# The second mixture of a four-layer kernel: two sends signalled apart, fill products ahead of and during the first fetch, first rows rounded in halves, and the dense expert by 512 columns

## The reference, cut to what matters

```
logits = xf @ w_g
topv, topi = top_k(logits, 2)
full = full_like(logits, -1e9).at[arange(N)[:, None], topi].set(topv)
probs = softmax(full)
capacity = 640                       # int(2 * 1.25 * 2048 / 8)
rank = cumsum(one_hot(topi)) - 1     # first choices of all tokens, then second ones
mask = mask * (rank < capacity)
exp_batches = einsum('nec,nd->ecd', sec_mask, xf)
h = gelu(einsum('ecd,edh->ech', exp_batches, c_fc))    # 128 -> 512
exp_out = einsum('ech,ehd->ecd', h, c_proj)            # 512 -> 128
out = einsum('nec,ecd->nd', cb, exp_out)
```

## Time and profile before

| | before |
|---|---|
| median of 3 runs | 578.73 us (578.64 to 579.26) |
| the profiled execution | 577.52 us |
| its span, first to last instruction | 575.7 us |
| PE busy | 492.8 us (86%) |
| DVE busy | 323.8 us (56%) |
| POOL busy | 242.2 us (42%) |
| ACT busy | 241.1 us (42%) |

### The profile page before, as it was taken

How to read it: one execution, slowest core, us unless ns; L and a number is a source line. 1 busy time by engine, 2 the same in 40 slices (tenths; PEclk the granted TensorE clock), 3 DMA queues, 4 the chain that set the end, 5 groups by cost and what they waited for, 6 DMA issues and landing times.

```text
span 575.7 us, 9196 instructions
## 1 busy us (share of the span) xinstructions
PE 492.8 (86%) x3294; PEld 396.8 (69%) x3294; DVE 323.8 (56%) x1125; ACT 241.1 (42%) x477; POOL 242.2 (42%) x354
## 2 busy tenths in 40 slices
PE   2799893779779977987995499999899899999997
PEld 2558483769456726684884299998653778799997
DVE  4866427845896733688741146642775944433334
ACT  2653744324245541345560054421545295344440
POOL 5771866455335012366777515663760340000000
PEclk9799897559758997995598699999999999999999
DMA  9999710311850066700011212113500000000002
GB/s 279 336 201 206 249 58 12 99 38 32 291 172 1 0 172 166 213 1 0 29 52 49 83 54 81 40 37 126 179 2 0 2 1 2 0 1 1 1 2 73
DMA packets 56861, 48.04 MB, mean 83 GB/s; under 512 B 6082, under 2 KB 47240, under 8 KB 56688
## 3 DMA queue, kind: packets, MB, share of 16 engines
q1 hardware_dynamic: 53728, 42.06, 26.2%
q0 software_dynamic: 2656, 4.88, 2.7%
q10 hardware_dynamic: 432, 0.52, 0.3%
HBM read 35.21 MB, written 12.82 MB: 83 GB/s over the span
## 4 chain that ended last, share of the span: by engine, by line
PE 60%; DVE 24%; POOL 6%; issue 5%; DMA 3%; ACT 2%; ACTq 0%; POOLq 0%; DVEq 0%; SPq 0%
PE ps L1248 10%; PE ps L1186 6%; DVE st L1628 5%; PE ps L1069 4%; PE ps L1071 4%; PE ps L1070 4%; POOL tok L2309 3%; PE ps L822 3%; PE ps L709 3%; PE ps L752 3%; PE ps L762 2%; DVE mv L1631 2%; PE ps L845 2%; PE ps L825 2%; DVE mx L1666 2%
## 5 line engine op out<-in xcount | busy, mean ns | idle before, releaser
L2058 DVE SCALAR_TENSOR_TENSOR x<-ps,gate,x 128x128 f32<-128x128 f32 x128 | 36.0, 344 | 54.8 <-PE ps L1248 54.8
L1248 PEld LDWEIGHTS ps<-moe_w,big 128*128 128x128 f32 x512 | 61.1, 192 | 3.9 <-issue 1.7
L1515 ACT ACTIVATE big<-ps,col 128x512 f32<-128x512 f32 x64 | 42.2, 689 | 48.2 <-PE ps L1071 48.1
L1248 PE MATMUL ps<-moe_w,big 128*128 128x128 f32 x512 | 61.4, 275 | 0.9 <-DVE x L2047 0.9
L2400 POOL DMA_INDIRECT res<-qT,dest x43 | 42.2, 981 | 41.2 <-DVE qT L2033 26.7
L709 PE MATMUL ps<-con,xn 128*128 128x128 f32 x148 | 29.3, 332 | 28.1 <-ACT xn L1451 15.3
L1507 ACT ACTIVATE big<-ps 128x320 f32<-128x320 f32 x56 | 24.3, 439 | 59.2 <-PE ps L1071 59.0
L709 PEld LDWEIGHTS ps<-con,xn 128*128 128x128 f32 x148 | 20.5, 171 | 38.8 <-DVE xn L1646 34.8
L2199 POOL TENSOR_SCALAR rstd<-mv 128x4 f32<-128x4 f32 x36 | 9.2, 256 | 80.5 <-DVE mv L1631 79.5
L1363 ACT ACTIVATE xT<-ps 128x512 f32<-128x512 f32 x41 | 24.1, 590 | 45.2 <-PE ps L709 45.2
L1186 PE MATMUL ps<-moe_w,big 128*128 128x128 f32 x344 | 41.3, 275 | 0.6 <-ACT big L1507 0.6
(11 more groups left out here) (345 smaller groups left out, 1197.7 us busy)
## 6 DMA issues: line engine op xcount, KB each, us to landing
ring<-in_ew SPq DMA_DIRECT2D x20, 256.0 KB, 4.7
moe_w<-in_m0w SPq DMA_DIRECT2D x16, 256.0 KB, 6.2
moe_w<-in_m2w SPq DMA_DIRECT2D x16, 256.0 KB, 5.8
tok<-zero SPq DMA_DIRECT2D x1, 2580.0 KB, 27.7
big<-tok SPq DMA_DIRECT2D x7, 322.5 KB, 2.8
res<-zero SPq DMA_DIRECT2D x1, 2048.0 KB, 28.6
moe_w<-in_ew SPq DMA_DIRECT2D x8, 256.0 KB, 5.7
big<-res SPq DMA_DIRECT2D x4, 512.0 KB, 5.7
```

What stands on the lines that cost most here:

```text
L1248: last = mm(ps[7 - i % 2 if i >= B else 6 + i % 2][:, cols(c)], big[:, FC * (e % 2) + f, i % B, cols(c)], w[:, e, F + P * f:F + P * f + P] ...
L1515: A(big[:, 2 * (e % 2) + f, t, :], bank[:, :], ACT.Gelu, bias=V("m3b1", 2 * e + f)).then_inc(h_act, 1)
L2058: last = v.scalar_tensor_tensor(out=x[:, C * t + c, :], in0=bank[:, cols(c)], scalar=gate[:, C * t + c, e:e + 1], in1=x[:, C * t + c, :], ...
```

## The change

- **Sends.** The last two of the 32 sends count on a semaphore of their own (`sent_last`, which is `r_ld[1]`). SP and POOL wait for both, as before for the one. PE waits for the first 30 sends, issues 9 constant products, waits for the last two, issues 10 more, and 4 more after the first transposes.
- **First rows.** The first expert's five transposes go two to `ps0` and three to `ps1`. DVE rounds and subtracts the first 256 columns, ACT rounds the other 384, DVE subtracts them. Each half has its own signal, and the first expert's products and gelus are of 256 and 384 columns instead of 320 and 320. The transposes of the second group no longer wait for the whole of DVE's first group, only for both halves.
- **Dense expert.** The first layer is one fp32 product of 512 columns per unit instead of three fp32r passes. The second layer of tiles 0 to 2 is 4 products of 512 columns instead of 16 of 128, which leaves it by dimension. Hence 12 transposes (`whole_turned`) bring it back, and DVE adds it to `x` straight from PSUM (`whole_add`), all of it ahead of the first fetch. Tile 3 keeps the old second layer. ACT's four roundings of `x`, DVE's four remainders and POOL's split of expert 0's weights are gone.
- **Count.** DVE sums the 16 first-choice matrices (`oh_sum`), and PE multiplies the sum once instead of 16 products.
- Two small ones: `minus_half` is merged into `zeroed`, and four diagonals move from `xT` to `kr_w`.

```diff
+LAST = 2
+SENT = 16 * (2 * B * C - LAST + 2)
+SENT_LAST = 16 * (LAST + 2)
...
             def count_second():
-                for c in range(nb):
-                    mm(ps[1][:, 0:(nb + 1) * E], ones[:, :], bc(oh[:, c, :], [P, nb + 1, E], [1]), start=c == 0, stop=False)
                 pe.wait_ge(oh_ready, 2 * B + 1)
+                mm(ps[1][:, 0:(nb + 1) * E], ones[:, :], bc(oh_sum[:, :], [P, nb + 1, E], [1]), start=True, stop=False)
...
                 def hidden(t):
-                    pe.wait_ge(low_ready, t + 1)
+                    if not late:
+                        pe.wait_ge(xT_ready, turns(rows, t))
                     for f in range(4):
                         if t >= 1:
                             pe.wait_ge(h_act, n["h"] - 3)
-                        product(ps[2 + f][:, :], w1_high["m2"][:, 0, cols(f)], w1_low["m2"][:, 0, cols(f)],
-                                qTR[:, t, :], whole_low[:, t % 2, :])
+                        elif f % 2:
+                            pe.wait_ge(xT_ready, turns(rows, (f + 1) // 2))
+                        mm(ps[2 + f][:, :], moe_w[:, 0, cols(f)], xT[:, t, :], start=True, stop=True).then_inc(h_mm, 1)
...
+                def results_by_dim(t, units):
+                    for f in range(4):
+                        last = mm(ps[6 + t % 2][:, :], moe_w[:, 0, 512 + P * f:512 + P * f + P], hid[:, t % 2, f, 0:S],
+                                  start=f == 0, stop=f == 3)
...
+            def whole_turned():
+                for t in range(B - 1):
+                    pe.wait_ge(gy_sb, done0["whole"] + min(t + 2, B - 1))
+                    if t >= 2:
+                        pe.wait_ge(whole_added, t - 1)
+                    for c in range(C):
+                        last = nc.tensor.transpose(ps[7 - t % 2][:, cols(c)], whole_y[:, C * t + c, :], ident)
+                    last.then_inc(whole_tok, 1)
...
                 if name == "m2":
+                    whole_turned()
                     pe.wait_ge(sent, SENT)
-                    keep_busy(ps[7], BUSY // 2 + 2)
+                    keep_busy(ps[2], BUSY // 2 + 2)
+                    pe.wait_ge(sent_last, SENT_LAST)
+                    keep_busy(ps[2], BUSY // 2 + 3)
...
                 turn_group(0)
+                if name == "m2":
+                    keep_busy(ps[2], 4)
                 units = hidden(0)
...
+            def whole_add(t):
+                dve.wait_ge(whole_tok, t + 1)
+                for c in range(C * t, C * t + C):
+                    i = v.scalar_tensor_tensor(out=x[:, c, :], in0=ps[7 - t % 2][:, cols(c - C * t)], scalar=have[:, c:c + 1], in1=x[:, c, :],
+                                               op0=ALU.mult, op1=ALU.add)
+                i.then_inc(whole_added, 1)
...
+                    if name == "m2" and g == 0:
+                        link(v.tensor_copy(xg_high[:, 0, 0:FIRST], ps[0][:, 0:FIRST]))
+                        v.tensor_tensor(xg_low[:, 0, 0:FIRST], ps[0][:, 0:FIRST], xg_high[:, 0, 0:FIRST].bitcast(F32), ALU.subtract).then_inc(gT_s, 1)
+                        dve.wait_ge(first_high, 1)
+                        v.tensor_tensor(xg_low[:, 0, FIRST:], ps[1][:, 0:a["cap"] - FIRST], xg_high[:, 0, FIRST:].bitcast(F32), ALU.subtract).then_inc(gT_s, 1)
...
                 if name == "m2":
+                    act.wait_ge(gT_m, PLACED["m0"]["groups"] + 1)
+                    A(xg_high[:, 0, FIRST:], ps[1][:, 0:a["cap"] - FIRST], ACT.Identity).then_inc(first_high, 1)
...
-                                      oob_is_err=False).then_inc(sent, 16)
+                                      oob_is_err=False).then_inc(sent if j < 2 * B * C - LAST else sent_last, 16)
```

More of the change, by code:

```diff
@@ L369, in build @@
         oh = sb("oh", [P, 2 * B * C, E], BF16)
+        oh_sum = sb("oh_sum", [P, E], BF16)
         tri = sb("tri", [P, P], BF16)
@@ L544, in build @@
             a["N"] = a["cap"] // a["pieces"]
+        FIRST, HALVES = 2 * P, 2
+        piece = lambda name, i, j: slice((0, FIRST)[j], (FIRST, PLACED[name]["cap"])[j]) if name == "m2" and i == 0 else slice(j * PLACED[name]["N"], (j + 1) * PLACED[name]["N"])
         done0["last"] = done0["m2"] + PLACED["m2"]["n"] * PLACED["m2"]["nb"]
@@ L1075, in whole_expert @@
                 pe.wait_ge(loaded, 32 * E)
-                pe.wait_ge(split, 8)
-                pe.wait_ge(x_high, B)
+                rows = n["turn"] - 1
                 def hidden(t):
-                    pe.wait_ge(low_ready, t + 1)
+                    if not late:
+                        pe.wait_ge(xT_ready, turns(rows, t))
                     for f in range(4):
@@ L1101, in whole_expert @@
                 if late:
-                    results(B - 1, hidden(B - 1))
+                    results_by_token(B - 1, hidden(B - 1))
                     return
@@ L1161, in hidden @@
                                 pe.wait_ge(h_act, n["h"] - 3)
-                            tokens = slice(at + j * N, at + (j + 1) * N)
+                            tokens = slice(at + piece(name, i, j).start, at + piece(name, i, j).stop)
+                            N = tokens.stop - tokens.start
                             if name == "m2":
+                                if i == 0 and f == 0:
+                                    pe.wait_ge(gT_s, g0 - HALVES + j + 1)
                                 high, low = w1_high[name][:, e, cols(f)], w1_low[name][:, e, cols(f)]
@@ L1183, in results @@
                             pe.wait_ge(gy_sb, done0[name] + q - 1)
+                        if q < 2 and name == "m2":
+                            pe.wait_ge(whole_added, B - 1)
                         o = ps[6 + q % 2][:, cols(0)]
@@ L1218, in stage @@
                     if t == 0:
-                        pe.wait_ge(split, 16)
+                        pe.wait_ge(split, PLACED["m2"]["n"] + E)
                     for f in range(2):
@@ L1360, in stage @@
                         A(xT[:, t, :], ps[2 * t + 1][:, :], ACT.Identity).then_inc(xT_ready, 1)
-                        A(qTR[:, t, :], ps[2 * t + 1][:, :], ACT.Identity).then_inc(x_high, 1)
                     else:
@@ L1987, in group @@
                         dve.wait_ge(h_mm, units0[name] + 4 * a["pieces"] * eg * (g - 1))
-                    for j in range(0, gb_, 4):
+                    if name == "m2" and g == 0:
[3 more added lines that the diff above has]
+                        v.tensor_tensor(xg_low[:, 0, FIRST:], ps[1][:, 0:a["cap"] - FIRST], xg_high[:, 0, FIRST:].bitcast(F32), ALU.subtract).then_inc(gT_s, 1)
+                    for j in range(gb_ if name == "m2" and g == 0 else 0, gb_, 4):
                         m = min(4, gb_ - j)
@@ L2105, in _ @@
             second_largest(False)
+            with_sum = oh[:, 0:nb, :].rearrange("p c e -> p e c")
+            with nc.allow_low_precision(reason="whole numbers up to 16"):
+                v.tensor_reduce(oh_sum[:, :], with_sum, AX.X, ALU.add)
             first_largest(lg2[:, :, :], oh[:, nb:2 * nb, :], slice(0, nb))
@@ L2127, in _ @@
             link(v.tensor_tensor(have[:, 0:nb], gb[:, 0:nb, 0], gb[:, nb:2 * nb, 0], ALU.add))
-            whole_low_of(2)
-            whole_out(0)
-            whole_low_of(3)
-            for t in range(1, B - 1):
+            for t in range(B - 1):
                 whole_out(t)
             prepared("L3")
+            for t in range(B - 1):
+                whole_add(t)
+            dve.wait_ge(whole_added, B - 1)
             evacuate("m2", 1)
@@ L2259, in stage @@
                         for e in (2 * t, 2 * t + 1):
-                            split_expert(mix, w, width, e)
+                            if name == "L3" or e >= PLACED["m2"]["whole"]:
+                                split_expert(mix, w, width, e)
                 return stage
@@ L2406, in _ @@
             g_.memset(attT[:, :], 0.0).then_inc(zeroed, 1)
-            g_.memset(half[:, :], -0.5).then_inc(minus_half, 1)
-            pool.wait_ge(minus_half, 1)
+            g_.memset(half[:, :], -0.5).then_inc(zeroed, 1)
+            pool.wait_ge(zeroed, 3)
             pool.wait_ge(ld_c, 32)
```

61 lines of the change are left out of this document (30 added, 31 removed).

## The result

The changed kernel took 575.66 us, median of 5 runs (574.72 to 577.50), the kernel before 578.64 us (5 runs, 578.30 to 579.26). The ratio is 0.9948, with a 95% interval of 0.9925 to 0.9972: 3.0 us faster. The forecast was 576.1 us, 575.0 to 578.1.

A forecast was written before the change was run, and what follows sets the result against it. POOL's sends bound the kernel up to 321.8 us, then PE. A 3.3 us earlier second group less 0.6 for tile 3 gave 2.7 us: 578.73 - 2.7 = 576.03, forecast 576.1 us, range 575.0 to 578.1.

The forecast's parts named there:

- Sends and transposes: Second mixture's start: fill begins after the 30th send, clock rises 4.0 us later, transposes start at 325.4 against 325.67.
- the lower bound: Transposes behind the last send: no earlier than 325.0, because of the fetch; the second group then gains 3.7 us.
- The late rise: Rival at the fill: clock rises 2 to 3 us later, net gain 1.2 to 1.7 us, 577.2; chance 0.17.
- the bound 326.9: Transposes' start if the rise comes 3 us later: 16.4 products are slow, the second group gains 1.8 us.
- First rows: First expert's halves: first product at about 327.1 against 328.89, second group 3.3 us earlier.
- Dense expert: Tiles 0 to 2: 24 products take 20.6 us against 19.2, PE free before 319.3; effect taken as zero.
- the rival: Whole dense stage at 1.2 GHz: free until PE comes after 321.3; all 24 products slow, near 587; chance 0.05.
- Tile 3: Dense expert's last tile: four fp32 products take 3.44 us against 2.86, so 0.6 us is taken off the gain.
- The rest at zero: Roundings, remainders, split and 15 counting products lie beside POOL's chain of sends: zero gain.
- Sum: Whole kernel: 3.3 - 0.6 = 2.7 us gained.
- What would have shown it wrong: Signs include transposes later than 4.5 us behind the landing, or first sum less than 2 us earlier.
- listed for right: Signs include fill 2.5 us before the landing, first product about 5.4 behind it, first sum released by constant products.

The follow-up runs named there:

- clock-kept kernels: Changed kernel with 8 more constant products ahead of the wait for the 30th send: 575.17 us, ratio 0.9929; three variants of this: 0.9944, 0.9929, 0.9925.
- the second profile of the changed kernel: Changed kernel run again with no edit, against the kernel before: 576.64 us, ratio 0.9942.
- dense edit alone: Changed kernel with the second mixture's start as before, also called dense edit only: 579.73 us, ratio 1.0019 to the kernel before.
- Count only: Kernel before with one summed one-hot in place of the sixteen counting products: 580.94 us (1 run).
- dense edit only, again: Second timing of the changed kernel with the second mixture's start as before: 579.28 us, ratio 0.9997 to the kernel before.
- one signal: Changed kernel with 9 constant products behind the signal of all 32 sends, instead of 9 and 10 behind two signals: 577.54 us, ratio 0.9971 to before.
- rows whole: Changed kernel with the first group of rows rounded whole and products of 320 columns: 576.86 us, ratio 0.9967 to the kernel before.

## Why the prediction was right, step by step

**Sends and transposes: right, at the lower bound.** The rise came 3.2 us after the start of the fill where I took 4.0, and the transposes stood 3.08 us behind the landing where I took 3.6 (325.4 against 321.82). The clock-kept kernels show that the bound of the fetch, 325.0 or 3.2 us, was well read: 2.97 to 3.05. What the step did not weigh enough is that the fill is a bet: started slow, nineteen products ended 3.08, 3.34, 4.48 or 5.17 us behind the landing in four profiles.

**The late rise: a rival that happened, in single executions.** I gave it 0.17 and the bound 326.9, which is 5.1 behind the landing; the second profile of the changed kernel has 5.17. It costs 2.1 us in the sum. How many of the timed runs had it is not known, since only a profiled one shows the moment. The spread of the runs is not explained by it: the first profile, with the early rise, is of the slowest of its five runs. The Trainium skill, TensorE: Matmul & The Clock Gate, Part 1, gives half a microsecond either way for the moment; the runs here spread from 2.7 to 5.8 us behind the start of the constant products, so the measurement decides against that figure for this place.

**First rows: right.** The halves take 1.75 us from transposes to first product (I had 1.7, before 3.22). Idle time ahead of the first product is 0.18 us (0.2 to 0.3). The products of the first expert run at 0.12 to 0.18 us. The second group is 3.68 us earlier where the sum had 3.3: the term was 0.4 too small, and that is the half microsecond of the transposes.

**Dense expert: mechanism right.** Windows of the changed kernel's first profile, where it starts at 292.64:

```profile
293.00:294.00 1.00, 1.00 (x2) 0.46 (x2) 0.93 (x5) 0.28 (x1) 0.97 (x1) 0.50 0.20 66
294.00:295.00 1.00, 1.00 (x2) 0.32 (x1) 0.90 (x5) 0.27 (x1) 0.70 (x1) 0.62 0.20 66
```

The clock was low for its first 2.1 us, as feared in the rival, and it took 21.7 us to the key products (23.2 in the first profile of the dense edit alone) against 20.6 at full clock. PE was still through at 319.0, 3.2 us before it was wanted. Tile 3 costs 0.58 us more, as predicted 0.6. The estimate from the Trainium skill's four passes (FP8 and Floating Point Precision, TensorE Precision Notes) was 0.95, and the trace does not bear it out. Of these 0.58 only 0.33 came off the gain: tile 3 starts 3.83 us earlier and the first sum 3.50. Before, the fetch set the first sum, and PE had the rest to spare. The term was 0.3 too large.

**The rest at zero: wrong by 0.3 us,** the step "lie beside POOL's chain of sends: zero". One send of 1.35 us becomes 0.97. Count only shows that the summed count alone does it, by moving DVE against POOL; in the changed kernel DVE's subtractions, beside which the send was long, are gone as well, so there either edit could be the cause.

**Sum.** 3.5 us behind the landing and 0.3 ahead of it, in place of 2.7. The medians say 3.0 [0.28% to 0.75%, 1.6 to 4.3 us]. The rest, 0.8 us, is less than executions differ by elsewhere. That the median fell within 0.4 us of the forecast is in part luck: at the loop, at tile 3 and at the sends the working left out 0.3 to 0.4 us of gain each, all to the same side, and the two profiles of the changed kernel gained 3.5 and 1.4 us behind the landing.

**One price was added up wrongly,** that of the rival in which the whole dense stage is slow. If 9.5 us of lateness eat the whole gain, 20.6 us leave 11.1 on top of 578.7, near 590 and not 587. The rival did not come, and neither forecast nor range rests on it.

**What would have shown it wrong** was there in one of two profiles of the changed kernel, the second: transposes later than 4.5 us behind the landing (5.17), and a first sum less than 2 us earlier (77.93 against 79.32, 1.39). In the first profile all was as listed for right: fill 2.6 us ahead of the landing, first product at 4.83 (5.4 predicted), the first sum released by constant products.

## What to carry to other kernels

When an engine's wait is filled so that its clock is high for what follows, keep the clock rather than raise it: eight products ahead of the wait (34 with the old dense expert) made the end of the fill a matter of the data (2.97 to 3.05 us in four profiles), while nineteen that had to raise the clock ended anywhere from 3.08 to 5.17. Split the first tile of a pipeline so that its first product waits for a part of the rounding. Taking the halves away cost 1.57 us in the profile and taking the early fill away 1.05, but by the medians it was 0.2 and 0.9 us with intervals that overlap, so which of the two is worth more is not shown. And compare profiles from a common event next to the change: here both spans were equal, with 3.5 us gained in between.

## What the runs showed that I had not expected

- Against the first profile of before, an execution loses up to 1.3 us at 15 to 20 us, in products that take twice as long, or nothing there. Near 230 us it loses up to 0.75 us, and in one profile (dense edit only, again) it gains 1.4; this was not traced to a row. The first send started anywhere from 276.8 to 280.3 us.
- From the first sum to the end it took 174.2 to 176.5 us in the profiles, with nothing changed there. In the longest, the granted clock was 0.83 in one stretch of 20 us where the changed kernel's first profile has 1.00 (windows of the changed kernel, second profile and first):

```profile
440.00:460.00 20.00, 18.27 (x118) 12.53 (x117) 17.73 (x43) 5.01 (x10) 4.66 (x11) 0.83 0.00 1
```

```profile
440.00:460.00 20.00, 18.26 (x137) 12.26 (x136) 18.27 (x49) 6.21 (x13) 5.00 (x12) 1.00 0.00 1
```

- How long an idle TensorE keeps its clock differs as much as the rise. In the second profile of the changed kernel it went idle at 318.58 and the clock fell at 319.7, 1.1 us later, and in the first of dense edit only it was 1.1 us again (idle from 318.01). In the first profile of the changed kernel, in one signal and in rows whole it fell 3.0 to 3.2 us after PE had gone idle. So the waits of 1.05 to 1.58 us at an unbroken clock, seen above in rows whole and in the kernels with a kept clock, are no proof that such a wait is safe. Windows of the second profile:

```profile
318.00:319.00 1.00, 0.58 (x4) 0.34 (x4) 1.00 (x5) 0.00 (x0) 0.95 (x1) 1.00 0.16 51
319.00:320.00 1.00, 0.00 (x0) 0.00 (x0) 0.87 (x4) 0.00 (x0) 0.74 (x1) 0.85 0.23 70
```
